# Row maxima of the first attention unit inside the last batch of the projection stage, and the first two units' q, k and v loaded between that stage's stores

## What is computed

```
q = (x @ wq).reshape(B, S, H, hd).transpose(0, 2, 1, 3)
k = (x @ wk).reshape(B, S, H, hd).transpose(0, 2, 1, 3)
v = (x @ wv).reshape(B, S, H, hd).transpose(0, 2, 1, 3)
scores = jnp.einsum('bhqd,bhkd->bhqk', q, k) / jnp.sqrt(jnp.asarray(hd, x.dtype))
scores = jnp.where(causal, scores, jnp.finfo(x.dtype).min)
attn = jax.nn.softmax(scores, axis=-1)
ctx = jnp.einsum('bhqk,bhkd->bhqd', attn, v)
...
def ternarize(W, threshold):
    absW = jnp.abs(W)
    delta = threshold * jnp.max(absW)
    mask = absW > delta
```

## Time and profile before

| | |
|---|---|
| device time, median of 3 | 2650.17 us (2649.89 to 2651.44) |
| profiled execution, device time | 2649.13 us |
| its span | 2647.1 us |
| mean granted TensorE clock | 0.962 |
| PE busy | 2425.0 us, 92% |
| DVE, ACT, POOL busy | 46%, 31%, 34% |
| HBM traffic | 96 GB/s over the span |

### The profile page before, as it was taken

One profiled execution on the slowest core, in us unless ns is written; L12 is line 12 of the kernel. 1 busy time (PEld: TensorE's weight loads), 2 busy tenths in 40 slices (PEclk: granted clock), 3 DMA queues, 4 the chain that ended last, 5 costly groups with the idle time before them and its releaser, 6 DMA issues. The chain is left out here.

```text
span 2647.1 us, 39886 instructions
## 1 busy us (share of the span) xinstructions
PE 2425.0 (92%) x12832; PEld 1797.7 (68%) x12832; DVE 1218.3 (46%) x2491; ACT 819.4 (31%) x1371; POOL 911.5 (34%) x1099
## 2 busy tenths in 40 slices
PE   7999699999999968599999994799999979999997
PEld 5888455555555436478888883588888858888886
DVE  3333477777777759611111112767677362111121
ACT  3222055555555531043344432111101112222221
POOL 0000156556556545233333332525153222222221
PEclk9999699999999988799999997899999989999999
DMA  6665735545544335400100103403212061000000
GB/s 246 226 226 191 175 91 126 120 117 122 126 117 117 80 109 190 147 17 32 48 32 32 32 16 111 148 33 126 95 63 95 9 202 49 32 32 32 32 33 32
DMA packets 154489, 255.29 MB, mean 96 GB/s; under 512 B 9648, under 2 KB 47536, under 8 KB 153904
## 3 DMA queue, kind: packets, MB, share of 16 engines
q1 hardware_dynamic: 137712, 208.20, 26.3%
q0 software_dynamic: 6144, 25.17, 2.9%
q10 hardware_dynamic: 10560, 20.97, 2.3%
HBM read 161.50 MB, written 92.27 MB: 96 GB/s over the span
## 5 line engine op out<-in xcount | busy, mean ns | idle before, releaser
L736 DVE CUSTOM_DVE_ANT_0 p_junk<-psum,p_causal 128x896 bf16<-128x896 f32 (+7 forms) x512 | 370.6, 752 | 159.2 <-PE psum L596 149.9
L699 ACT ACTIVATE p_probs<-psum 128x512 f32<-128x512 f32 (+1 forms) x640 | 331.3, 554 | 325.4 <-PE psum L607 319.9
L1130 POOL TENSOR_TENSOR p_h_lo<-p_h,p_h_hi 128x512 fp32r<-128x512 f32 x128 | 165.1, 1290 | 338.3 <-ACT p_h_hi L1159 338.3
L607 PE MATMUL psum<-p_qst,p_kst 98*128 98x512 f32 (+3 forms) x768 | 245.9, 384 | 17.3 <-ACT p_probs L699 10.9
L607 PEld LDWEIGHTS psum<-p_qst,p_kst 98*128 98x128 f32 x768 | 131.5, 190 | 170.3 <-ACT p_probs L699 84.8
L519 POOL TENSOR_SCALAR_AFFINE_SELECT p_probs<-p_probs 128x128 f32<-128x128 f32 x512 | 145.9, 305 | 263.8 <-ACT p_probs L699 263.0
L596 PE MATMUL psum<-p_kst,p_qst 96*128 96x512 f32 (+5 forms) x768 | 206.0, 369 | 20.5 <-DMA p_kst<-k_parts 17.0
L1762 POOL CAST p_h<-p_h 128x512 fp32r<-128x512 f16 x128 | 91.7, 716 | 372.9 <-ACT p_h L1786 372.9
L845 PE MATMUL psum<-p_xT_hi,tern 128*128 128x512 f32 x512 | 206.2, 403 | 1.4 <-DVE p_xT_lo L1224 1.4
L1195 PE MATMUL psum<-tern,p_h_hi 128*128 128x512 f32 x512 | 203.0, 397 | 2.2 <-POOL p_h_lo L1130 2.2
L845 PE MATMUL psum<-p_xT,p_w_hi 128*128 128x512 f32 x512 | 203.2, 397 | 0.7 <-ACT p_xT L1773 0.7
(11 more groups left out here) (174 smaller groups left out, 4764.2 us busy)
## 6 DMA issues: line engine op xcount, KB each, us to landing
p_qst<-q_parts SPq DMA_DIRECT2D x96, 256.0 KB, 4.6
p_kst<-k_parts SPq DMA_DIRECT2D x96, 256.0 KB, 6.9
q_parts<-p_qk_out SPq DMA_DIRECT2D x32, 512.0 KB, 2.8
k_parts<-p_qk_out SPq DMA_DIRECT2D x32, 512.0 KB, 2.8
ffn_x<-x SPq DMA_DIRECT2D x12, 1024.0 KB, 5.6
p_x<-in_x_t POOLq DMA_DIRECT2D x8, 1024.0 KB, 6.4
p_raw<-in_f_w POOLq DMA_DIRECT2D x8, 1024.0 KB, 7.9
v_rows<-p_v_out SPq DMA_DIRECT2D x32, 256.0 KB, 4.8
```

The costliest lines, as they stand in the source:

```text
L607: mm = pe.matmul(ST_BANKS[st % 2][:, col:col + CH - q0], kst[s][0:KD + 2, g, j * P:(j + 1) * P], qst[s][0:KD + 2, c, g, q0:CH], start=True ...
L699: act.activation(probs[:, n % 2, g, col:CH], ST_BANKS[st % 2][:, col:CH], ACT.Exp, scale=SM_SCALE).then_inc(p_ready, 1)
L736: dve.tensor_tensor_reduce(halves_of(junk[:, which, 0:n]), scores, halves_of(causal[:, SEQ - n:SEQ]), 1.0, FLOOR, ALU.add, ALU.max, rowmax ...
L1130: pool.tensor_tensor(h_lo[:, m % 2, :], h[:, m % 2, :], f32(h_hi[:, m % 2, :]), ALU.subtract).then_inc(hl_done, 1)
```

## The change

**Loads.** `phase_attention` no longer starts with the loads of units 0 and 1. In the projection stage SP now waits after batch 0 for all of its stores to land. In batch 1 it issues one load of unit 0 behind each of the first 13 stores (12 of q and k, one of v), in batch 2 the same for unit 1. The buffers `kst`, `qst`, `vs` and the others that both stages now share are allocated outside of them, at the other end of the memory. The semaphores of attention that count these loads are preset.

**Entries.** In batch 3 PE computes the 32 entries and the turn of half 0 of unit 0 between its projection matmuls, in banks 0 and 1. A short entry takes one of the two banks in turn, a long one takes both. In the q and k groups of the first half one entry stands in the middle of a group and one behind it; the four v groups carry the other nine. In the second half, each of the eight q and k groups has one in its middle. DVE reduces them between its subtractions. PE waits before an entry until the banks that it needs are read.

**Room and raw pieces.** The stage's own buffer for raw pieces is gone: it uses the junk buffer and v's second buffer, halves of the old size. All 16 pieces are read in batches 0 and 1, two pairs per half, instead of 8 in four batches. The staging of weights has 3 slots instead of 4. The memsets of the mask and of the ones rows move to POOL at the head of the projection stage, behind the first load of x. The maximum over partitions is taken with two PE transposes in batch 2 and a DVE reduction, no longer on POOL.

In what follows names that begin with p1_ or p2_ are printed as p_.

The core of the diff:

```diff
+    def load_qk(self, eng, q_dram, k_dram, u, s, c, r, of_q, loaded):
+
+        dst = self.qst[s][:, c, :, :] if of_q else self.kst[s][:, :, c * CH:(c + 1) * CH]
+        src, part = (q_dram, (0, 0, 1)[r]) if of_q else (k_dram, (0, 1, 0)[r])
+        view = src[u, part].rearrange("(h d) t -> d h t", d=HD)[:, :, c * CH:(c + 1) * CH]
+        eng.dma_start(f32(dst[r * HD:(r + 1) * HD, :, :]), view).then_inc(loaded, 16)
...
+    def reduce_rows(self, dve, bank, which, c, tile, g):
+
+        n = P * (CT * c + tile + 1)
+        flat = len(bank.shape) == 2
+        view = lambda ap: ap if flat else ap.rearrange("p (a n) -> p a n", a=2)
+        col = g * CT + tile
+        return dve.tensor_tensor_reduce(view(self.junk[:, which, 0:n]), bank, view(self.causal[:, SEQ - n:SEQ]), 1.0, FLOOR,
+                                        ALU.add, ALU.max, self.rowmax[:, c, col:col + 1])
...
-        stage = sb("p1_stage", [P, 4, KT * D // 2], F32)
...
+        stage = sb("p1_stage", [P, 3, KT * D // 2], F32)
+        raw = (first.junk[:, :, :].rearrange("p a n -> p (a n)").bitcast(F32), first.vs[1][:, :, :].rearrange("p t e -> p (t e)"))
...
+        ENTRIES = [(0, t, g) for t in range(CT) for g in range(HPG)] + [(1, t, g) for t in range(CT) for g in range(HPG)]
+        TURN = PER_UNIT + 5
+        ENTRIES.insert(TURN, (0, None, None))
+        QK_PLACES = [[2 * o, 2 * o + 1] for o in range(2 * GROUPS)]
+        V_PLACES = [[16, 17], [18, 19], [20, 21, 22], [23, 24]]
+        LAST_PLACES = [[25 + o] for o in range(2 * GROUPS)] + [[]] * CT
+        PLACES = [QK_PLACES + V_PLACES, LAST_PLACES]
...
+        def bank_of(k):
+            c, tile, _ = ENTRIES[k]
+            if tile is None:
+                return psum[0:2 * PER_UNIT, 0, 0:P]
+            n = P * (CT * c + tile + 1)
+            return psum[:, k % 2, 0:n] if c == 0 else psum[:, 0:2, 0:n // 2]
...
+                build(1, pool.memset(first.causal[:, :], 0.0))
+                tri = first.causal[:, SEQ - P:SEQ]
+                build(2, pool.affine_select(out=tri, in_=tri, compare_op=ALU.is_ge, fill=FLOOR, base=0,
+                                            pattern=[[-1, P]], channel_multiplier=1))
+                for s in range(2):
+                    build(3 + s, pool.memset(f32(first.kst[s][96:128, :, :]), 1.0))
...
+                def load_pieces(b, c, k):
+                    for n in range(2):
+                        pool.wait_ge(piece_done, 8 * b + 4 * c + 2 * k + n + 1)
                         pool.sem_inc(passed, 1)
-                        n = raw_v[c].shape[2]
-                        pool.dma_start(raw[:, c, :].rearrange("p (k n) -> p k n", k=n), raw_v[c][b]).then_inc(raw_loaded[c], 16)
+                        pool.dma_start(raw[n], raw_v[n][bass.ds(4 * b + 2 * c + k, 1)].rearrange("o p m -> p (o m)")).then_inc(raw_loaded[n], 16)
+
+                def body(b, early, last):
+                    for c in range(2):
+                        if early:
+                            load_pieces(b, c, 0)
                         if not (c and last):
                             pool.wait_ge(xt_lo, 8 * b + 4 * c + 4)
                             pool.sem_inc(passed, 1)
                             load_x(b + c, 1 - c)
-                batches(pool, body)
+                        if early:
+                            load_pieces(b, c, 1)
...
+                def load_first(u, i):
+
+                    if i < QK_LOADS:
+                        first.load_qk(sp, q_dram, k_dram, u, u, i // 6, i % 3, i // 3 % 2 == 0, first_qk[u])
+                    elif i == QK_LOADS:
+                        first.load_v(sp, v_dram, u, u, first_v)
...
+                            if u is not None:
+                                load_first(u, i)
+                            i += 1
...
+                        if last and c == 0:
+                            sp.wait_ge(s_used, 2 + TURN + 1)
+                            first.load_max(sp, 0, 0, max_loaded)
...
+                stores(0, None)
+                all_stored(0)
+                stores(1, 0)
+                sp.wait_ge(piece_done, 2 + 2 * PIECES)
+                stores(2, 1)
+                stores(3, None, True)
+                all_stored(3)
...
+                def scores(k):
+                    c, tile, g = ENTRIES[k]
+                    if k == 0:
+                        pe.wait_ge(first_qk[0], 16 * QK_LOADS)
+                        pe.wait_ge(const_done, CONSTS)
+                        pe.wait_ge(bound_step, 2)
+                    pe.wait_ge(s_used, k + 1 if k < PER_UNIT else k + 2)
+                    if tile is None:
+                        pe.wait_ge(nm_ready, 1)
+                        first.turn(pe, bank_of(k), c, ident).then_inc(s_ready, 1)
+                        return
+                    n = P * (CT * c + tile + 1)
+                    keys = n if c == 0 else n // 2
+                    for k0 in range(0, n, keys):
+                        bank = psum[:, k % 2 if c == 0 else k0 // keys, 0:keys]
+                        mm = pe.matmul(bank, first.qst[0][0:3 * HD, c, g, tile * P:(tile + 1) * P],
+                                       first.kst[0][0:3 * HD, g, k0:k0 + keys], start=True, stop=True)
+                    mm.then_inc(s_ready, 1)
...
+                                if last and kt == 1:
+                                    for k in PLACES[c][o][:1]:
+                                        scores(k)
...
                             mm.then_inc(proj, 1)
-                batches(pe, body)
+                            if last:
+                                for k in PLACES[c][o][1:]:
+                                    scores(k)
+                        if not early and not last and c == 0:
+                            pe.wait_ge(bound_step, 1)
+                            for n in range(2):
+                                mm = pe.transpose(psum[:, 0, n * P:(n + 1) * P], w_max_cols[:, n, :], ident[:, :])
+                            mm.then_inc(w_max_turned, 1)
...
+                            if last:
+                                for k in PLACES[c][j]:
+                                    maximum(k)
...
+        loaded = [[sem(f"p2_loaded{s}_{c}", LOADS) for c in range(2)] for s in range(2)]
+        v_loaded = [sem(f"p2_v_loaded{s}", 16) for s in range(2)]
+        max_loaded = [sem("p2_max_loaded0", 1 + MAX_LOADS), sem("p2_max_loaded1", 1)]
...
-                build(1, pool.memset(causal[:, :], 0.0))
-                tri = causal[:, SEQ - P:SEQ]
-
-                build(2, pool.affine_select(out=tri, in_=tri, compare_op=ALU.is_ge, fill=FLOOR, base=0,
-                                            pattern=[[-1, P]], channel_multiplier=1))
-                build(3, pool.memset(ones[:, :], 1.0))
-                for s in range(2):
-                    build(4 + s, pool.memset(f32(kst[s][96:128, :, :]), 1.0))
-                for n in range(2):
-                    build(6 + n, pool.partition_all_reduce(bound[:, n, 0:1], w_max[:, n:n + 1], P, bass.bass_isa.ReduceOp.max))
-                build(8, pool.tensor_scalar(bound[:, :, 1], bound[:, :, 0], TERN, None, ALU.mult))
-                build(9, pool.tensor_scalar(bound[:, :, 2], bound[:, :, 1], -1.0, None, ALU.mult))
+                build(1, pool.memset(ones[:, :], 1.0))
...
-                load(0, 0, 0)
-                load(0, 0, 1)
-                load_v(0, 0)
-                load(1, 1, 0)
-                load(1, 1, 1)
-                load_v(1, 1)
-                load_max(0, 0, LEAD_TURNED)
-                load_max(0, 1, LEAD + turned(1))
+                load_max(0, 1, turned(1))
...
-                for k, e in enumerate(FIRST_ROUND):
-                    if e in (SHORT[0], LONG[0]):
-                        pe.wait_ge(loaded[0][e[1]], LOADS)
-                    score_entry(k, lead_banks[k], e, -1, 1)
-                pe.wait_ge(const_done, CONSTS)
+                pe.wait_ge(const_done, 1)
```

More of the change, by code:

```diff
@@ L10 @@
 from contextlib import ExitStack
+from dataclasses import dataclass
 import numpy as np
@@ L130, in build_constants, with load_v, load_max, negate_hi @@
     return ident
-def phase_qkv0(nc, psum, x_t, wq, wk, wv, q_dram, k_dram, v_dram, ffn_w, w_max):
+@dataclass
+class Scores:
+    kst: object
+    qst: object
+    vs: object
+    junk: object
+    rowmax: object
+    negmax: object
+    max_rows: object
+    causal: object
+    bound: object
+    def load_qk(self, eng, q_dram, k_dram, u, s, c, r, of_q, loaded):
[3 more added lines that the diff above has]
+        eng.dma_start(f32(dst[r * HD:(r + 1) * HD, :, :]), view).then_inc(loaded, 16)
+    def load_v(self, eng, v_dram, u, s, loaded):
+        eng.dma_start(self.vs[s][:, :, :], v_dram[u].rearrange("(t p) e -> p t e", p=P)).then_inc(loaded, 16)
+    def load_max(self, eng, s, c, loaded):
+        for part in range(2):
+            src = self.max_rows[part * HPG * CT:(part + 1) * HPG * CT, c, :]
+            row = 3 * HD + part
```

(25 more changed lines are left out.)

192 lines of the change are left out of this document (114 added, 78 removed).

## The result

| | before | after |
|---|---|---|
| median of the runs | 2651.30 us (10 runs, 2649.89 to 2653.04) | 2657.81 us (10 runs, 2652.20 to 2659.46) |
| ratio, 95% interval | | 1.0022, 1.0013 to 1.0030 |
| profiled execution | 2649.13 us | 2652.20 us |
| its span | 2647.1 us | 2650.5 us |

The kernel became slower, by some 0.2%; 2625 (2614 to 2640) had been predicted. It compares runs made side by side and isn't the quotient of the medians.) The profiled execution of the changed kernel is its fastest; what the others, with a median 5.6 us above it, probably lose comes with experiment 8.

What follows compares the result with a forecast made beforehand. PE was taken as the bound in the projection stage, idling in a hole before attention. Terms -44.7 + 11.0 + 6.6 - 0.7 + 2.7 + 0 = -25.1 from 2649.13 gave 2624.0, median 2625 us; range 2614 to 2640.

Steps and rivals of the forecast that it cites:

- other work that moves: Projection stage: DVE's reductions, SP's wait for stores and max-row loads fit into existing slack; nothing in the sum.
- E: Batches 1 and 2: while loads are queued, all DMA traffic moves at 222 GB/s; slower, 2661 us; chance 0.05.
- Rival C: Batch 3: two banks couple PE to DVE, each of 33 entries holding PE 0.5 us; 2641 us; chance 0.10.
- removed: Between PE's last projection matmul and attention's first transposed score: the whole stretch goes, -44.7 us.
- entries, turn, transposes in batch 3: PE in batch 3: score entries, turn, two transposes and one immediate wait add 11.0 us, bounds 8 to 19.
- border: Projection to attention: last v store, stage closing and POOL's semaphore presets still hold PE, +6.6 us, bounds 5.2 to 8.
- start of the program: First batch: x lands earlier, but PE waits for wk's second half and its clock falls again; +2.7 us, -2 to +6.
- slow start of attention: Attention's first steps: low clock lasts 7 us instead of 9.5; -0.7 us, bounds 0 and -2.2.
- loads behind stores: Batches 1 and 2: extra DMA traffic delays stores, but output buffers and PSUM banks keep it from PE; 0 us.
- rival B: Batches 1 and 2: DMA overflow reaches PE, costing 5 to 10 us; about 2632 us; chance 0.13.
- the wait for p_w_lo of 3 to 4 us near 20 us: Program start: sign of a right forecast, PE waiting 3 to 4 us for weights; no such wait would mean wrong.
- fails as a whole: Projection-attention border: forecast declared failed if the stretch up to the first transposed score shrinks by less than 20 us.

Runs made afterwards that it cites:

- experiment 8: Changed kernel with 58 idle instructions at the start of DVE's program, plus a fourth staging place for the weights: 2623.72 us, ratio to before 0.9895.
- kernel with 88: Changed kernel plus 88 idle semaphore increments at the start of DVE's program: 2627.18 us, ratio to before 0.9913.
- the kernels with 58 and 88: Changed kernel plus 58 or 88 idle semaphore increments at the start of DVE's program: 2629.45 and 2627.18 us.
- the kernels with filler: Changed kernel plus 40 to 112 idle semaphore increments at the start of DVE's program, three weight places: 2627.18 to 2666.55 us.
- with 40: Changed kernel plus 40 idle semaphore increments at the start of DVE's program: 2666.55 us, ratio to before 1.0042 to 1.0076.
- with 48: Changed kernel plus 48 idle semaphore increments at the start of DVE's program: 2666.19 us, ratio to before 1.0037 to 1.0074.

## Why the prediction was wrong

**The step that failed** is "other work that moves". It looked at where instructions are carried out and how long they take, and put the rest at nothing. That DVE's program had grown ahead of the attention loop, by 40 instructions, was there to be counted. It shifted an unchanged loop over the end of a piece, and that alone is worth +28 us: 2678.71 in the kernel before, and from 2629.45 and 2627.18 back up to 2657.81 in the changed one. None of the rivals had it. E, the one on the slower side, named DMA traffic in batch 1, and these batches last nearly as long as before: batch 1 takes 65.25 us between two of PE's branches in both kernels, batch 2, from its first matmul to that of batch 3, 65.5 us against 65.3. Rival C is out too, with 0.4 us of waits in batch 3. E came nearest in its time (2661) and had another mechanism.

**The terms of the sum**, against the kernels where the loop isn't hurt:

| term | predicted, us | measured, us |
|---|---|---|
| removed | -44.7 | -44.7, by definition |
| entries, turn, transposes in batch 3 | +11.0 (8 to 19) | +11.0 (210.5 - 199.5) |
| border | +6.6 (5.2 to 8) | +5.6 |
| start of the program | +2.7 (-2 to +6) | +6.3 (88.15 - 81.81); +0.9 in the changed kernel's profile; +1.0 with four places |
| slow start of attention | -0.7 (0 to -2.2) | +1.4 (kernel with 88, from the first transposed score to the end of the span; +0.7 of it up to the loop's first branch on DVE; -0.3 to +4.4 in the other kernels with short jumps) |
| loads behind stores | 0 | 0 |
| the jump of DVE's loop | not in the sum | +28 |

Without the last line they give -20.4, and 2649.13 - 20.4 = 2628.7, plus the 1.04 to the median 2629.8; the kernels with 58 and 88 measured 2629.45 and 2627.18. The measured terms cut the span of the kernel with 88 into parts, so that they add up to it is no proof; what they show is which term was off. With the loop in a good place the changed kernel would have lain inside the stated range, at 2627 to 2632 us. The start was mis-sized: its mechanism was the one described (wk's second half waits for a slot, PE for it, and the clock falls a second time), but in the kernel with 88 the half came at 24.4 and not at 22 (at 21.44 in the changed kernel's profiled execution). The slow start of attention went the other way: the low clock lasts 11.0 us behind the first transposed score with 88, 10.8 in the changed kernel and 9.5 before, where 7 had been assumed. The border had been put too dear, mostly because the thirteen increments of POOL start within 0.9 us (297.9 to 298.8) and not 0.17 apart.

The rule of the Trainium skill (TensorE: Matmul & The Clock Gate, Back-to-back issue gap) that would have made the entries 7.8 instead of 9.3 us finds no support: they cost 9.7. The one of the Trainium skill on queues (DMA: Bandwidth & Descriptors, Queues, rings and completion order) that was weighed in rival B did no harm here: PE was busy for 40.00 of 40 us with the DMA share at 1.02. That nothing of before shows loads and stores mixed was a misreading: in the attention stage SP issues loads of k at 407.74 and a store at 413.94, in one queue. And the lower end of the range needs attention's -2.2 as well; the three bounds that are named for it give 2616, not 2614.

Of the signs that were named, the gap of 6 us with a transposed score at its end (5.57), the unchanged batches, the DMA share near 1 in batch 1 (1.02), and the 11 us of batch 3 came true; the wait for p_w_lo of 3 to 4 us near 20 us was 1.2 at 23.9 in the changed kernel's profile and 2.9 to 5.0 in the kernels with filler. That the forecast fails as a whole "if the stretch up to the first transposed score shrinks by less than 20 us" was too narrow a watch: it shrank by 27, and the time was lost elsewhere.

## What to carry to other kernels

Count the instructions of each engine ahead of its long loops, before and after an edit: a DVE loop of 331 instructions lies in three or in four pieces of 128 by its place, and here 40 instructions more ahead of it tipped each jump back from 0.3 to 4.7 us. Where the pieces end can't be told from the count alone, since in these programs the ends don't lie at multiples of 128; the recurring packets show it. In a profile this is an "issue" wait at the loop's first operation together with instruction packets that recur in every turn; some tens of idle instructions, put where the engine has nothing to do (93 ns each here, done by 11.0 us where its first work is at 12.0), move the loop to a better place. Compare kernels only with their loops in like places, or a good change is thrown away for a reason that isn't its own.

## What the runs showed that was not expected

- A packet on queue 14 has 8 KB, one on queue 8 has 16 KB. Queue 8 looks like PE's: in the straight code behind the loop of the changed kernel PE carries out 246 to 271 matmuls and weight loads from one packet to the next (898.67 to 958.75 us). PE's loop of this stage, with some 580 matmuls and as many weight loads a turn, has no packet of queue 8 between 405 and 860 us in either kernel.
- A DVE stall of 4.3 us costs PE some 2.5 us of waiting and then, in five of six turns, 3.4 or 6.8 us at half clock, which together can be almost as dear as the waits (12 us at most against 16.0).
- Not settled: with a piece's end 5 or 13 instructions into the loop the jump itself is shorter (3.7 to 4.3 us) and the sum dearer by some 9 us than with the end at 53. The traces show what is dearer: with 40 DVE stops twice in a turn (3.65 and 1.76 us in the turn shown), with 48 its first reduction comes 6.29 us late in one piece in the second turn; PE's waits for DVE come to 20.6 and 27.9 us over the six turns, against 16.0, and both have 6.8 us at half clock in each of the six. Why a piece's end so early in the loop does this is open. 1.9 us between the last store of attention and the end of the span, more than before, weren't looked into.
